# Inverse roots of both token norms as exp of minus half a logarithm, and no dummy products ahead of the turned probabilities

## The reference

```python
x = x + _L0_conv_ref(_gn(x), ...)        # attention with learnt sampling offsets, softmax over 16 keys
t = _to_tokens(x)                        # (8, 256, 32)
t = t + _L1_attn_ref(_ln_t(t))           # scores = t t^T, softmax over 256 keys, weights t
t = t + _L1_ffn_ref(_ln_t(t), ...)       # router over 16 experts, top 8 tokens of each, two layers
x = _from_tokens(t, x)

def _ln_t(v, eps=1e-05):
    m = jnp.mean(v, axis=-1, keepdims=True)
    s = jnp.var(v, axis=-1, keepdims=True)
    return (v - m) / jnp.sqrt(s + eps)
```

## Time and profile before

| | us |
|---|---|
| median of 3 runs | 65.5 |
| lowest and highest of them | 65.31, 67.98 |
| the profiled execution, in all | 65.6 |
| its span in the profile | 63.8 |
| busy in the span: PE, PEld | 53.4, 43.8 |
| busy in the span: DVE, ACT, POOL | 38.4, 34.3, 21.3 |
| dummy products (L649), 220 of them, busy | 16.0 |
| table loads, 8 of them | 10.3 |

### The profile page before, as it was taken

How to read it: one execution, slowest core, us unless ns; L and a number is a source line. 1 busy time by engine, 2 the same in 40 slices (tenths; PEclk the granted TensorE clock), 3 DMA queues, 4 the chain that set the end, 5 groups by cost and what they waited for, 6 DMA issues and landing times.

```text
span 63.8 us, 1448 instructions
## 1 busy us (share of the span) xinstructions
PE 53.4 (84%) x584; PEld 43.8 (69%) x584; DVE 38.4 (60%) x93; ACT 34.3 (54%) x70; POOL 21.3 (33%) x44
## 2 busy tenths in 40 slices
PE   3994996996996999999989758689996993999830
PEld 3993885954785899998979655433684682788710
DVE  3278598918499893699701751899968265240720
ACT  0910052969999040069867794995889249001020
POOL 3005389875788999002400000012000950000000
PEclk9999999999999999999999999999999999999999
DMA  0899711100000000000000000000000000000004
GB/s 0 224 192 279 204 51 47 55 10 0 0 0 0 0 10 0 0 0 0 0 0 10 5 5 0 0 0 0 0 0 0 10 0 0 0 0 0 0 10 154
DMA packets 3926, 2.02 MB, mean 32 GB/s; under 512 B 2640, under 2 KB 3792, under 8 KB 3920
## 3 DMA queue, kind: packets, MB, share of 16 engines
q1 hardware_dynamic: 1424, 1.37, 7.1%
q10 hardware_dynamic: 2496, 0.57, 4.2%
HBM read 1.67 MB, written 0.26 MB: 30 GB/s over the span
## 4 chain that ended last, share of the span: by engine, by line
PE 45%; DVE 17%; ACT 16%; POOL 7%; DMA 6%; issue 5%; ACTq 1%; DVEq 0%
DMA wts<-weights 6%; PE ps L730 4%; ACT L505 4%; ACT e_tok L601 4%; PE ps L826 3%; PE ps L774 3%; PE ps L723 3%; PE ps L795 3%; PE ps L752 3%; DVE taps L969 2%; POOL w_smp L465 2%; PE ps L810 2%; PE ps L649 2%; PE ps L901 2%; DVE off L971 2%
## 5 line engine op out<-in xcount | busy, mean ns | idle before, releaser
L649 PE MATMUL ps<-zeros 128*128 128x128 bf16 x220 | 16.0, 231 | 1.0 <-DVE zeros L946 1.0
L649 PEld LDWEIGHTS ps<-zeros 128*128 128x128 bf16 x220 | 14.6, 105 | 1.9 <-DVE zeros L946 1.0
L505 ACT ACT_TABLE_LOAD x8 | 10.3, 1283 | 1.8 <-PEq L1149 1.6
L601 ACT ACTIVATE e_tok<-ps,cst 128x1024 f32<-128x1024 f32 (+1 forms) x5 | 4.4, 941 | 1.1 <-PE ps L819 0.9
L378 POOL TENSOR_TENSOR c_scaled<-ln_c,e_sum 128x256 f32<-128x256 f32 x1 | 0.6, 621 | 11.7 <-DVE e_sum L1062 11.7
L1062 DVE TENSOR_REDUCE e_sum<-e_tok 128x4 f32<-128x1024 f32 x3 | 3.6, 1217 | 0.4 <-ACT e_tok L601 0.3
L1000 DVE COPY_PREDICATED ps<-over,ps 128x608 f32<-128x608 uint32 (+1 forms) x4 | 3.1, 777 | 0.8 <-PE ps L702 0.7
L418 POOL TENSOR_TENSOR wblk<-wts,cst 128x256 f32<-128x256 f32 x3 | 2.3, 763 | 3.7 <-DMA wts<-weights 3.7
L826 PE MATMUL ps<-e_tok,t 128*32 128x256 f32 x32 | 3.1, 385 | 0.2 <-ACT e_tok L601 0.2
L702 PE MATMUL ps<-rpe_blk,minus_hat_rel 128*32 128x168 f32 x64 | 2.8, 316 | 0.5 <-DVE minus_hat_rel L996 0.5
L488 POOL TENSOR_TENSOR o_n<-ln_c,e_rec 128x256 f32<-128x256 f32 x2 | 1.2, 620 | 5.9 <-DVE e_rec L1080 5.9
(11 more groups left out here) (180 smaller groups left out, 125.7 us busy)
## 6 DMA issues: line engine op xcount, KB each, us to landing
w_sb<-weight ACTq DMA_DIRECT2D x1, 256.0 KB, 6.0
w_sb<-weight SPq DMA_DIRECT2D x1, 256.0 KB, 5.3
x_nat<-x_rows SPq DMA_DIRECT2D x8, 32.0 KB
wts<-weights SPq DMA_DIRECT2D x1, 192.5 KB, 4.9
cst<-shape_consts SPq DMA_DIRECT2D x1, 192.0 KB, 4.0
x_sb<-x_rows SPq DMA_DIRECT2D x1, 128.0 KB, 2.5
x_sb<-x_rows ACTq DMA_DIRECT2D x1, 128.0 KB, 2.7
cst<-shape_consts SPq DMA_DIRECT2D x1, 128.0 KB, 5.0
```

The source lines that it names most:

```text
L505: nc.scalar.activation(warm[:, n:n + 1], zeros[:, 0:1], func)
L601: return nc.scalar.activation(dst, scores, ACT.Exp, bias=const("bound"))
L649: mm(bank(n_bank, P), zeros[:, :], zeros[:, :], start=True, stop=True)
```

## The change

The standard deviation tile becomes `ln_log`. In both norms the square root on ACT and the reciprocal on DVE give way to two activations on ACT: the natural logarithm of the summed squares, and the exponential of minus half of it, which is the inverse root. ACT waits for its own semaphore between the two. DVE waits for `ln_rstd_ready` instead of `ln_std_ready` and only multiplies. Four of the eight `load_table` calls are gone (both Sqrt ones beside the norms, and both Exp ones behind them), and the one ahead of the first softmax asks for Ln, of 0 + 1, instead of Exp. Sqrt at the start, Gelu twice and this one are left. Last, `BUSY["d_prob_ready"]` is 0 instead of 12.

```diff
--- before.py
+++ after.py
@@ -40,7 +40,7 @@
 
 BUSY = {
     "xn_ready": 45, "off_ready": 22, "off_blk_ready": 28, "w_smp_ready": 20, "xs_ready": 8,
-    "d_prob_ready": 12, "prob_copied": 3, "t1_ready": 20, "t1_copied": 7, "t2_ready": 12,
+    "d_prob_ready": 0, "prob_copied": 3, "t1_ready": 20, "t1_copied": 7, "t2_ready": 12,
     "picked_ready": 16, "pooled_ready": 9, "hidden_ready": 3, "out2_ready": 15,
 }
 QK_SCALE = float(DH) ** -0.5
@@ -235,7 +235,7 @@
         ln_c = sb("ln_c", [P, 2, NHALF, B, C])
         ln_sq = sb("ln_sq", [P, NHALF, B, C + 1])
         ln_ss = sb("ln_ss", [P, 2, NHALF, B])
-        ln_std = sb("ln_std", [P, 2, NHALF, B])
+        ln_log = sb("ln_log", [P, 2, NHALF, B])
         ln_rstd = sb("ln_rstd", [P, 2, NHALF, B])
         c_scaled = sb("c_scaled", [P, NHALF, B, C])
         u_sq = sb("u_sq", [P, NHALF, B, C + 1])
@@ -339,8 +339,8 @@
         d_exp_ready, d_rec_ready = sem("d_exp_ready"), sem("d_rec_ready")
         d_prob_ready = [sem(f"d_prob_ready{h}") for h in range(NHALF)]
         prob_turned, prob_copied, att_done = sem("prob_turned"), sem("prob_copied"), sem("att_done")
-        ln_c_ready, ln_sq_ready, ln_ss_ready, ln_std_ready = (
-            sem("ln_c_ready"), sem("ln_sq_ready"), sem("ln_ss_ready"), sem("ln_std_ready"))
+        ln_c_ready, ln_sq_ready, ln_ss_ready, ln_log_ready, ln_rstd_ready = (
+            sem("ln_c_ready"), sem("ln_sq_ready"), sem("ln_ss_ready"), sem("ln_log_ready"), sem("ln_rstd_ready"))
         t1_ready, t1_turned = sem("t1_ready"), sem("t1_turned")
         t1_copied = [sem(f"t1_copied{t}") for t in range(NT)]
         scores_done, exp_ready, e_sum_ready = sem("scores_done"), sem("exp_ready"), sem("e_sum_ready")
@@ -498,11 +498,11 @@
             act.dma_start(wts[:, 0:WEIGHT_CUT], weights_in[:, 0:WEIGHT_CUT]).then_inc(weights_loaded[0], 16)
             warmed = [0]
 
-            def load_table(func):
+            def load_table(func, bias=0.0):
 
                 n = warmed[0]
                 warmed[0] += 1
-                nc.scalar.activation(warm[:, n:n + 1], zeros[:, 0:1], func)
+                nc.scalar.activation(warm[:, n:n + 1], zeros[:, 0:1], func, bias=bias)
 
             act.wait_ge(zeros_set, 1)
             load_table(ACT.Sqrt)
@@ -554,7 +554,7 @@
 
             act.wait_ge(off_done, 4)
             nc.scalar.activation(half_tanh[:, :], off_ps[2], ACT.Tanh, scale=0.5).then_inc(half_tanh_ready, 1)
-            load_table(ACT.Exp)
+            load_table(ACT.Ln, 1.0)
 
             act.wait_ge(shifts_done, 1)
             nc.scalar.activation(win[:, :, :], row_ps[0][:, :, 0:IMG + 1], ACT.Copy).then_inc(win_copied, 1)
@@ -573,7 +573,6 @@
             copy_heads(1, v_ready)
             act.wait_ge(d_sub_ready, 2)
             nc.scalar.activation(d_exp[:, 1], d_sub[:, 1], ACT.Exp).then_inc(d_exp_ready, 1)
-            load_table(ACT.Sqrt)
             act.wait_ge(vo_done, 1)
             nc.scalar.activation(vo_c[:, :, :, :], voc_ps, ACT.Copy).then_inc(vo_copied, 1)
             for h in range(NHALF):
@@ -588,10 +587,15 @@
                 nc.scalar.activation(ln_sq[:, h, :, 0:C], centred, ACT.Square,
                                      scale=float(C) ** -0.5).then_inc(ln_sq_ready, 1)
                 nc.scalar.activation(ln_c[:, 0, h], centred, ACT.Copy).then_inc(ln_c_ready, 1)
-            for h in range(NHALF):
-                act.wait_ge(ln_ss_ready, h + 1)
-                nc.scalar.activation(ln_std[:, 0, h], ln_ss[:, 0, h], ACT.Sqrt).then_inc(ln_std_ready, 1)
-            load_table(ACT.Exp)
+            def inverse_root(k, h):
+
+                act.wait_ge(ln_ss_ready, NHALF * k + h + 1)
+                nc.scalar.activation(ln_log[:, k, h], ln_ss[:, k, h], ACT.Ln).then_inc(ln_log_ready, 1)
+                act.wait_ge(ln_log_ready, NHALF * k + h + 1)
+                nc.scalar.activation(ln_rstd[:, k, h], ln_log[:, k, h], ACT.Exp, scale=-0.5).then_inc(ln_rstd_ready, 1)
+
+            for h in range(NHALF):
+                inverse_root(0, h)
 
             act.wait_ge(t1_turned, 1)
             nc.scalar.activation(t1_t[:, 0], t1t_ps[0], ACT.Copy).then_inc(t1_copied[0], 1)
@@ -610,15 +614,12 @@
             for t in range(NT):
                 act.wait_ge(ot_done, t + 1)
                 nc.scalar.activation(ot[:, t], ot_ps[t], ACT.Copy).then_inc(ot_copied, 1)
-            load_table(ACT.Sqrt)
             for h in range(NHALF):
                 act.wait_ge(ln_c_ready, NHALF + h + 1)
                 nc.scalar.activation(u_sq[:, h, :, 0:C], ln_c[:, 1, h], ACT.Square,
                                      scale=float(C) ** -0.5).then_inc(ln_sq_ready, 1)
             for h in range(NHALF):
-                act.wait_ge(ln_ss_ready, NHALF + h + 1)
-                nc.scalar.activation(ln_std[:, 1, h], ln_ss[:, 1, h], ACT.Sqrt).then_inc(ln_std_ready, 1)
-            load_table(ACT.Exp)
+                inverse_root(1, h)
             act.wait_ge(t2_turned, 1)
             nc.scalar.activation(t2_t[:, 0], t2t_ps[0], ACT.Copy).then_inc(t2_copied[0], 1)
             act.wait_ge(g_done, 1)
@@ -1046,9 +1047,8 @@
                 dve.wait_ge(ln_sq_ready, h + 1)
                 reduce(ln_ss[:, 0, h], ln_sq[:, h], AX.X, ALU.add).then_inc(ln_ss_ready, 1)
             for h in range(NHALF):
-                dve.wait_ge(ln_std_ready, h + 1)
+                dve.wait_ge(ln_rstd_ready, h + 1)
                 dve.wait_ge(ln_c_ready, h + 1)
-                link(nc.vector.reciprocal(ln_rstd[:, 0, h], ln_std[:, 0, h]))
                 tt(t1[:, h], ln_c[:, 0, h], by_token(ln_rstd[:, 0, h]), ALU.mult).then_inc(t1_ready, 1)
 
             dve.wait_ge(t1_turned, 2)
@@ -1074,8 +1074,7 @@
                 dve.wait_ge(ln_sq_ready, NHALF + h + 1)
                 reduce(ln_ss[:, 1, h], u_sq[:, h], AX.X, ALU.add).then_inc(ln_ss_ready, 1)
             for h in range(NHALF):
-                dve.wait_ge(ln_std_ready, NHALF + h + 1)
-                link(nc.vector.reciprocal(ln_rstd[:, 1, h], ln_std[:, 1, h]))
+                dve.wait_ge(ln_rstd_ready, NHALF + h + 1)
                 tt(t2[:, h], ln_c[:, 1, h], by_token(ln_rstd[:, 1, h]), ALU.mult).then_inc(t2_ready, 1)
             nc.vector.reciprocal(e_rec[:, :, :], e_sum[:, :, :]).then_inc(e_rec_ready, 1)
             dve.wait_ge(t2_turned, NT)
```

## The result

The changed kernel took 77.3 us, the median of 4 runs (76.81 to 78.07), against 65.48 before: a ratio of 1.179 (95% interval 1.172 to 1.186). It is 11.8 us slower where 1.5 us faster was forecast.

The account below looks back on a forecast made before the run. No engine was taken as the bound: the kernel is one relay, and an edit is worth what it takes from that. Gains 0.65 + 0 + 0.19 + 0.72 = 1.56 gave 65.6 - 1.56 = 64.0 us, range 63.5 to 65.0.

Parts of the forecast that it names:

- table sets: At the Ln and Exp pairs: if they don't share a set, 10.3 us more, 74.3 to 75.6; chance 0.10.
- the clock rival: On TensorE: twelve dummies fewer let its clock fall, doubling the attention product's 2.04 us, 66.0 in all; chance 0.04.
- A: Twelve dummies ahead of the turned probabilities, removed: priced at 0.67 us, taken as 0.65, bounds 0.4 and 0.67.
- B: Sqrt load beside the twelve removed dummies and Exp load behind the first norm, removed: both hidden, gain nothing.
- C: First norm, root and reciprocal against log and exp: half 0 unchanged at 0.48 us, half 1 gains 0.19.
- D: Second norm without its Sqrt load: squares 0.45 and 0.42 us earlier, `t2[1]` gains 0.66, of which 0.24 from absent reciprocals.
- E: Exp load behind the second norm, removed: it held the chain by 0.06 us at the copy of `t2_t[0]`.

Follow-up runs that it names:

- the one-set kernel: The changed kernel with the dummy Ln load replaced by preloading the set natural_log_exp_and_others by name: 63.99 us, ratio to before 0.976.
- the repeat: The one-set kernel measured again, unchanged, beside two variants on the same chip: 64.27 us, ratio to before 0.983.

## Why the prediction was wrong

The step that failed is the one it calls a bet: that Ln and Exp work from one loaded set. It stood in the forecast as four table loads and in the rival "table sets" with a chance of 0.10. The runs put in its place: the named set holds both, but the loads placed for a dummy Ln and for each following activation never picked it. The evidence given for the forecast, Tanh behind Gelu's load, shows only that two functions can share the set that the first one brings in. The page named against the rival, of the Trainium skill ("ScalarE: Activation LUTs", section "Table sets: the hidden batching unit"), says that one set holds both and counts one load for ln then exp. The first half agrees with the one-set kernel; the count holds there (none beside eight activations) and not in the changed kernel (eight), so it isn't a property of the two functions but of what was loaded.

*The rival's own price* was 74.3 to 75.6 us, measured 77.3. Its 8 x 1.283 = 10.3 is right (10.4). The ninth load was to add up to 1.28 and added nothing, being issued ahead of its activation's wait in ACT's idle time. What it lacked is the clock: I let the clock rival hang on the dummies that were removed, and said that later waits only get shorter. In the table case they get 5 us longer, and that is where the clock fell, 2.4 to 2.8 us.

*A* was right: 0.67 in the trace, 0.76 measured, both inputs just in time. *B* (the loads beside stage A and behind the first norm cost nothing) was right too: with the dummies kept and these loads gone, `prob_t` does not move; and with the dummies gone the kernel that keeps both loads has the same intervals as the one-set kernel, 3.27 from the V products to the attention product and 1.79 from the end of `t1` to the first `e_tok`. *C* was half right. Ln, self-wait, Exp and handover took 0.48, as summed (in the one-set kernel 34.98 to 35.46), but the second half gained 0.05 and not 0.19: from the second square to the second product of `t1` it is 35.98 - 34.43 = 1.55 against 36.86 - 35.26 = 1.60. I had not counted that the product, which took over the reciprocal's place, now carries two waits. *D* was right to 0.01: the squares start at 45.34, behind `ln_c` (44.88 + 0.42) and not 1.5 us earlier, and from the start of `ln_c` to the second product of `t2` it is 47.07 - 44.88 = 2.19 against 48.61 - 45.77 = 2.84, a gain of 0.65. What it had wrong is the margin of PE's twelve dummies ahead of `t2`. I put their end at 47.30 + 0.67 = 47.97, but that start is the timeline's, where they take 0.83: they end at 48.13, 0.07 behind the first `t2` and not 0.09 ahead. In the one-set kernel they end at 47.24 and `t2` was due at 46.73 + 0.42 + 0.04 = 47.19, and the chain that ended last runs through PE alone there:

```profile
44.41 0.44 PE ps L832 x2
44.85 1.73 PE ps L866 x8
46.58 0.67 PE ps L650 x12
47.24 0.75 PE ps L874 x4
```

The loss is a few hundredths, but the next gain in the second norm would need these dummies gone first (not tried). *E* gave 0.03 of its 0.06, the router's product now starting 0.02 behind PE's own work (L877). The sum, 64.0, is what the one-set kernel measured, but by these steps its trace accounts for 0.67 + 0.05 + 0.65 + 0.03 = 1.40 of the 1.6 between the spans. The rest lies in the first 29 us (V products at 29.10 instead of 29.26), which differ by more than that between executions of one kernel (29.64 in the repeat), so part of the one-set kernel's hit was luck.

## What to carry to other kernels

An activation function that the profile has not yet shown is a bet on its table set. Count the loads in the build before believing any sum, and load the set that holds all of a stretch's functions by its name: a dummy activation loads a set that serves that one function, which need not be the shared one. Price a long wait twice, once for its length and once for the clock of what comes behind it on TensorE. A load that goes off the chain is worth only the distance to the next input, here 0.43 of its 1.5 us (from the start of the second `ot` copy to the squares 1.80 before, 1.37 in the one-set kernel).

## What I had not expected

- A table load runs ahead of the wait of the activation that needs it: 3.4 us ahead at L571, and at the second norm's first Ln at 52.73, right behind the squares, while the sum that this Ln reads is only being formed (from 52.41, 0.43 long). A forced load can therefore hide without any dummy activation if the engine is idle before it.
- Two semaphore waits on one DVE instruction kept it from overlapping the one before it: 0.52 between starts instead of 0.34.
- In the execution of 102.41 us of the kernel with both logarithms first, the granted clock is recorded as 1.00, yet the V products took 3.66 us against 2.05 in the kernel before and the attention product 3.68 against 2.04, while the table loads took their 1.28. That column doesn't tell all; what slowed PE there stays open.
